# Cached keys gathered during the first attention, transposed by VectorE, kept in DRAM and loaded transposed in the second

## What is computed

```python
x = x + _L1_attn_ref(_L1_cond_ref(x, lens, conv_w), w_qkv, w_o)          # attention 1: 32 heads, 8 key heads, d=128
x = x + _L1_ffn_ref(_L1_cond2_ref(x, Wq, Wk, Wv, Wo, ..., k_cache, v_cache, block_table, cache_seqlens), ...)

def _L1_cond2_ref(...):                                                   # attention 2: the same heads, with a paged cache
    q, k = _rope(_rmsnorm(x @ Wq.T), pos), _rope(_rmsnorm(x @ Wk.T), pos)
    v = x @ Wv.T
    kc = k_cache[block_table].reshape(bsz, 512, HK, D)                    # 16 pages of 32 keys for each sequence
    vc = v_cache[block_table].reshape(bsz, 512, HK, D)
    k_all, v_all = concat([kc, k], 1), concat([vc, v], 1)                 # 512 cached + 128 own keys
    scores = einsum('bqhd,bkhd->bhqk', q, repeat(k_all)) * SCALE          # cached keys at or past cache_seqlens masked
    o = einsum('bhqk,bkhd->bqhd', softmax(scores), repeat(v_all))
    return o @ Wo.T
```

## Time and profile before

| | |
|---|---|
| time, median of 3 runs | 2040.61 us (2037.54 to 2041.23) |
| time of the profiled execution | 2036.61 us, its span 2034.7 us |
| mean granted TensorE clock | 0.999 |
| busy: PE, DVE, ACT, POOL | 1986.8, 1534.6, 1324.8, 805.8 us |
| start of attention 2 (first L1629) | 889.02 us |

### The profile page before, as it was taken

One profiled execution on the slowest core, in us unless ns is written; L12 is line 12 of the kernel. 1 busy time (PEld: TensorE's weight loads), 2 busy tenths in 40 slices (PEclk: granted clock), 3 DMA queues, 4 the chain that ended last, 5 costly groups with the idle time before them and its releaser, 6 DMA issues.

```text
span 2034.7 us, 35876 instructions
## 1 busy us (share of the span) xinstructions
PE 1986.8 (98%) x12477; PEld 1695.1 (83%) x12477; DVE 1534.6 (75%) x3383; ACT 1324.8 (65%) x3796; POOL 805.8 (40%) x797
## 2 busy tenths in 40 slices
PE   6999999999999999999999999999999999999997
PEld 5778677888888888888888888888888888888774
DVE  6777764556656555687887888878878888888998
ACT  4676763445554544576776777767767767777785
POOL 3200015100000000056666666666666666666662
PEclk9999999999999999999999999999999999999999
DMA  7301101101201110121111111211211111112010
GB/s 261 99 28 48 53 1 73 62 32 37 68 32 39 56 53 1 58 79 31 62 53 31 63 51 32 71 44 36 80 32 63 53 32 62 53 31 83 26 31 37
DMA packets 45011, 108.62 MB, mean 53 GB/s; under 512 B 15634, under 2 KB 21010, under 8 KB 40354
## 3 DMA queue, kind: packets, MB, share of 16 engines
q1 hardware_dynamic: 28450, 72.74, 10.3%
q0 software_dynamic: 16384, 33.59, 5.6%
HBM read 103.14 MB, written 3.15 MB: 52 GB/s over the span
## 4 chain that ended last, share of the span: by engine, by line
PE 91%; DVE 4%; ACT 3%; issue 1%; DMA 1%; SPq 0%; DVEq 0%; ACTq 0%
PE PS L1662 10%; PE PS L1487 9%; PE PS L1430 9%; PE PS L1566 9%; PE PS L1674 8%; PE PS L1629 7%; PE PS L1647 7%; PE PS L1580 4%; PE PS L1443 4%; PE PS L1632 3%; PE PS L342 3%; PE PS L1458 3%; PE PS L1473 2%; PE PS L498 1%; PE PS L1465 1%; PE PS L1598 1%
## 5 line engine op out<-in xcount | busy, mean ns | idle before, releaser
L2528 POOL DMA_INDIRECT kcache<-in_kcache,rows x256 | 249.6, 975 | 533.1 <-DVE x_res L1829 462.4
L2536 POOL DMA_INDIRECT vcache<-in_vcache,rows x256 | 257.2, 1005 | 124.2 <-issue 58.4
L2002 DVE CUSTOM_DVE_ANT_0 pr<-PS,ffn_weights,sm 128x640 f32<-128x640 f32 x256 | 224.6, 885 | 87.5 <-PE PS L1632 87.5
L2387 ACT ACTIVATE pr<-pr,sm 128x640 f32<-128x640 f32 x256 | 212.5, 830 | 40.1 <-DVE sm L2002 39.3
L2018 DVE TENSOR_TENSOR prT_lo<-PS,prT_hi 128x512 fp32r<-128x512 f32 x320 | 209.2, 686 | 37.0 <-ACT prT_hi L2398 30.8
L2398 ACT ACTIVATE prT_hi<-PS 128x512 fp32r<-128x512 f32 x320 | 178.0, 597 | 61.1 <-PE PS L1647 60.5
L1647 PE MATMUL PS<-consts,pr 128*128 128x128 f32 x1280 | 172.3, 273 | 2.2 <-DVE prT_lo L2018 1.7
L1647 PEld LDWEIGHTS PS<-consts,pr 128*128 128x128 f32 x1280 | 149.7, 141 | 26.3 <-DVE prT_lo L2018 2.7
L2542 POOL TENSOR_TENSOR vcached_lo<-vcache,vcached_hi 128x512 fp32r<-128x512 f32 x64 | 83.7, 1308 | 218.7 <-ACT vcached_hi L2370 218.7
L1629 PE MATMUL PS<-kT_hi,qT_hi 128*128 128x320 f32 x512 | 154.4, 309 | 2.5 <-DVE sm L2002 1.2
L1629 PE MATMUL PS<-kT_lo,qT_hi 128*128 128x320 f32 x512 | 154.1, 309 | 0.0
(11 more groups left out here) (321 smaller groups left out, 6178.1 us busy)
## 6 DMA issues: line engine op xcount, KB each, us to landing
arena<-in_wqkv SPq DMA_DIRECT2D x16, 1536.0 KB, 6.5
arena<-in_wo SPq DMA_DIRECT2D x16, 1024.0 KB, 5.4
arena<-in_wcT SPq DMA_DIRECT2D x8, 1024.0 KB, 6.7
kcache<-in_kcache,rows POOLq DMA_INDIRECT x256
vcache<-in_vcache,rows POOLq DMA_INDIRECT x256
arena<-in_xT SPq DMA_DIRECT2D x8, 256.0 KB, 7.8
x_res<-in_x SPq DMA_DIRECT2D x1, 2048.0 KB, 13.5
ffn_weights<-in_alibi SPq DMA_DIRECT2D x2, 1024.0 KB, 7.1
```

What stands on the lines that cost most here:

```text
L2002: dve.tensor_tensor_reduce(pr2[:, h, :].rearrange("p (a n) -> p a n", a=2), PS[:, SCORE_BANK[h]:SCORE_BANK[h] + 2, 0:HALF], keymask[:, b, ...
L2387: act.activation(pr2[:, h, :], pr2[:, h, :], ACT.Exp, bias=nm2[:, h:h + 1], scale=-1.0, accum_out=rs2[:, h:h + 1]).then_inc(a2_ex, 1)
L2528: pool.indirect_dma_start(out=kcache[:, c, :], out_offset=None, in_=T["kcache"], in_offset=bass.IndirectOffsetOnAxis(ap=rows[:, g, b, c:c ...
L2536: pool.indirect_dma_start(out=vcache[:, c, :], out_offset=None, in_=T["vcache"], in_offset=bass.IndirectOffsetOnAxis(ap=rows[:, g, b, c:c ...
```

## The change

The cached keys are gathered during attention 1, in another order of rows, so that four 32x32-block transposes by VectorE make columns that a transfer can put in place; the transposed keys are written to DRAM by GpSimd (`turned_kept`) and loaded by SP into `kcache` in attention 2, already transposed.

- **GpSimd**: after the tables, `pool_turned_keys`: for each of the 64 items a gather of four indirect transfers into `key_pages` (two buffers), and a store of 256 KB from `key_turned` (two buffers, both in the part of `ffn_weights` where the masks come later). `pool_masks` follows it and now waits until all 64 stores have landed. In `pool_paged`, `load_keys` is gone, and `lo_of_cached_k` is now GpSimd's, once an item.
- **DVE**: `turn_keys` at the end of items 5 to 61 of attention 1, once an item and twice in every eighth one; `lo_of_cached_k` is gone from attention 2.
- **ACT**: `hi_of_cached_k` reads `kcache` in SBUF where it read bank 3. The first stands in item 62 of attention 1, before it stood in item 63.
- **PE**: no `turn_cached_k`. The output product of attention 2 is in bank 3 but for the last item; it waits for the second row maximum where it waited for the fourth; its other waits stay. The scores' wait for the adding of the product moved from head 0 to head 1.
- **SP**: four small transfers more at the start (page numbers in the other order, each read as 32 copies of 32 single numbers); four transfers of 64 KB an item in attention 2; the weights of attention 2 are issued between them.

```diff
+            for q in range(4):
+                sp.dma_start(key_page_i[q * 32:(q + 1) * 32, :],
+                             T["pages"].rearrange("c (b q) -> q (c b)", q=CHUNKS)[q, :].partition_broadcast(32),
+                             allow_slow_non_contiguous=True).then_inc(s_setup, 16)
...
+        FIRST_TURN, LAST_TURN = GH + 1, ITEMS - 3
+        def turns_in(i):
+            if not FIRST_TURN <= i <= LAST_TURN:
+                return range(0)
+            first = i - FIRST_TURN + (i - FIRST_TURN + B - 1) // B
+            return range(first, min(first + 1 + (i % B == FIRST_TURN), ITEMS))
+
+        def pool_turned_keys(pool):
+            def gather(n):
+                g, b = group_of(n)
+                wait(pool, s_kpt, n - 1)
+                wait(pool, s_kpg, 16 * CHUNKS * n)
+                for c in range(CHUNKS):
+                    pool.indirect_dma_start(out=key_pages[:, n % 2, c, :], out_offset=None, in_=T["kcache"],
+                                            in_offset=bass.IndirectOffsetOnAxis(ap=key_rows[:, g, c, b:b + 1], axis=0)
+                                            ).then_inc(s_kpg, 16)
+            def store(n):
+                pool.wait_ge(s_kpt, n + 1)
+                wait(pool, s_kps, 16 * n)
+                pool.dma_start(turned_kept[n, :, :, :].rearrange("r p n -> p r n"),
+                               key_turned[:, n % 2, :, :, :].rearrange("p r c n -> p r (c n)")).then_inc(s_kps, 16)
...
+            gather(0)
+            gather(1)
+            for n in range(ITEMS):
+                store(n)
+                if n + 2 < ITEMS:
+                    gather(n + 2)
+
         def pool_masks(pool):
-            pool.wait_ge(a1_xT, B)
+            pool.wait_ge(s_kps, 16 * ITEMS)
...
+            def load_keys(n):
+                wait(sp, a2_kcl, n)
+                for r in range(4):
+                    sp.dma_start(kcache[32 * r:32 * (r + 1), :, :],
+                                 turned_kept[n, r, :, :].rearrange("(a j) n -> j a n", j=32)).then_inc(a2_kg, 16)
+            load_weights2(0)
+            sp.wait_ge(s_kps, 16 * ITEMS)
...
-                elif i == ITEMS - 2:
-                    turn_cached_k(0)
...
                 if i + 1 < ITEMS:
-                    pe.wait_ge(a2_max, 4 * (i + 1) + 4)
+                    pe.wait_ge(a2_max, 4 * (i + 1) + 2)
                 for h in range(GH):
                     for j, (a, c) in enumerate(PARTS):
-                        mm = pe.matmul(bank(0), o2[a][:, h, :], w_out[c][:, h, :],
+                        mm = pe.matmul(bank(OUT_BANK[i + 1 == ITEMS]), o2[a][:, h, :], w_out[c][:, h, :],
...
-                    turn_cached_k(i + 1)
...
+            def turn_keys(n):
+                dve.wait_ge(s_kpg, 16 * CHUNKS * (n + 1))
+                wait(dve, s_kps, 16 * (n - 1))
+                dve.transpose(key_turned[:, n % 2, :, :, :].rearrange("p r c n -> p c r n"),
+                              key_pages[:, n % 2, :, :].rearrange("p c (r n) -> p c r n", r=4)).then_inc(s_kpt, 1)
...
             def hi_of_cached_k(n):
-                act.wait_ge(a2_kcT, n + 1)
-                act.activation(kT2[0][:, 0:CACHED], bank(3), ACT.Copy).then_inc(a2_kch, 1)
+                act.wait_ge(a2_kg, 16 * 4 * (n + 1))
+                wait(act, a2_sc, GH * n)
+                act.activation(kT2[0][:, 0:CACHED], kcache[:].rearrange("p c d -> p (c d)"), ACT.Copy).then_inc(a2_kch, 1)
...
+            def lo_of_cached_k(n):
+                pool.wait_ge(a2_kch, n + 1)
+                pool.tensor_tensor(kT2[1][:, 0:CACHED], kcache[:].rearrange("p c d -> p (c d)"), kT2[0][:, 0:CACHED],
+                                   ALU.subtract).then_inc(a2_kcl, 1)
```

More of the change, by code:

```diff
@@ L1249, in build @@
         SCORE_BANK = 0, 2, 4, 0
+        OUT_BANK = 3, 0
         QPARTS = KT + 1
@@ L1352, in sp_attentions, with load_weights2 @@
             sp.wait_ge(a1_wol, GH * G)
-            for g in range(G):
+            def load_weights2(g):
                 wait(sp, a2_wl, QPARTS * g)
@@ L1582, in project_kv @@
                 mm.then_inc(a2_kv, 1)
-            def turn_cached_k(n):
-                pe.wait_ge(a2_kg, 16 * CHUNKS * (n + 1))
-                if n == 0:
-                    pe.wait_ge(a1_kTc, ITEMS)
-                for c in range(CHUNKS):
-                    mm = pe.transpose(bank(3, P, c * P), kcache[:, c, :], ident)
-                mm.then_inc(a2_kcT, 1)
             def turn_q(n):
@@ L1610, in scores @@
                 for h in range(GH):
-                    if h == 0:
+                    if h == 0 and i == 0:
+                        pe.wait_ge(a1_max, ITEMS)
+                    if h == 1:
                         wait(pe, a2_acc, i - 1)
-                        if i == 0:
-                            pe.wait_ge(a1_max, ITEMS)
                     if h == 2 and i == 0:
@@ L1903, in step1 @@
                         lo_of_out_weights1(g, h)
+                for n in turns_in(i):
+                    turn_keys(n)
             def row_steps(step, inv, rows):
@@ L2522, in pool_paged @@
             ch = Chain(pool, s_chp, counted["pool"])
-            def load_keys(n):
-                g, b = group_of(n)
-                wait(pool, a2_kcT, n)
-                for c in range(CHUNKS):
-                    pool.indirect_dma_start(out=kcache[:, c, :], out_offset=None, in_=T["kcache"],
-                                            in_offset=bass.IndirectOffsetOnAxis(ap=rows[:, g, b, c:c + 1], axis=0)
-                                            ).then_inc(a2_kg, 16)
+            def lo_of_cached_k(n):
+                pool.wait_ge(a2_kch, n + 1)
+                pool.tensor_tensor(kT2[1][:, 0:CACHED], kcache[:].rearrange("p c d -> p (c d)"), kT2[0][:, 0:CACHED],
+                                   ALU.subtract).then_inc(a2_kcl, 1)
             def load_values(n, cs=range(CHUNKS)):
@@ L2628, in _ @@
             pool_tables(pool)
+            pool_turned_keys(pool)
             pool_masks(pool)
```

77 lines of the change are left out of this document (46 added, 31 removed).

## The result

The changed kernel takes 2085.06 us in the median of 4 runs (2082.49 to 2087.63), the kernel before 2039.64 in those rounds; the ratio is 1.0223, with a 95% interval from 1.0204 to 1.0242. The profiled execution has a span of 2079.7 us, 45.0 more than before.

What follows compares the result with a forecast made beforehand. TensorE was taken as the bound, but in attention 2 waiting for VectorE's low part. 2036.61 + 14.4 (junction) + 3 (start) - 1 (last items) = 2053.0, so a median of 2057, range 2050 to 2066 (0.62).

Steps and rivals of the forecast that it cites:

- Start: Kernel start: four new transfers of 1024 single numbers delay sequence 1's inputs; 3 us taken, between 0 and 38.
- My own rival with a start of 10 to 20 us: Kernel start: the new transfers cost 10 to 20 us instead of 3, total 2064 to 2074; chance 0.08.
- Gathers, transposes and stores in attention 1: Attention 1: VectorE's transposes fit its idle time and GpSimd's rounds fit 8.1 us each; cost taken as 0.
- Junction: Between the attentions: eight masks behind the last store delay item 0's factors, so attention 2 begins 14.4 us late.
- the slow landing: Junction: last store landing 5.4 us after issue, like the quantised weights', rather than 2.0; attention 2 then 18 us late.
- Steady item of attention 2: Attention 2: removing four transposes gains 0.00, since the output product still waits for VectorE's low part; 0.43 us becomes a wait.
- The 27 us of the rival: Attention 2: the removed transposes' 0.43 us is real, so 62 items save 27 us, giving 2030; chance 0.11.
- End: Last items of attention 2: the chain passes elsewhere there, so 1 us comes off (0 to 4).
- GpSimd as the bound of attention 1: Attention 1: a store costs 3.9 us, 64 rounds take 589 us against 522, 67 us slower, 2124; chance 0.10.
- Gathers slowing VectorE: Attention 1: gathers slow VectorE where GpSimd was idle, needing over 3.0 us an item; 2060 to 2078; chance 0.03.
- three signs of being wrong: Attention 2 item shorter by over 0.1 us, store issue over 2.8 us, or item 0's factors ready before 895.
- What would show it: Expected signs, among them: sequence 1's wait at 26.01 grows about 3 us; items of attention 1 keep their length.

Runs made afterwards that it cites:

- The runs with the steps: Changed kernel with the 1024 row steps stored as eight transfers of 128: 2106.80 us; with their one store moved behind attention 2's third load of keys: 2078.80 us.
- the masks apart: Changed kernel with GpSimd making mask 0 ahead of the last store and the other seven one by one in items 0 to 6 of attention 2: 2071.80 us.
- The needless transposes: Changed kernel with four transposes of a constant put in each item of attention 2 where the turns of the cached keys stood: 2083.18 us.
- the kernel before with the moved low part: Kernel before with only VectorE's low part of the last output moved ahead of the fourth row maximum: 2043.33 us, ratio 1.0002.

## Why the prediction was wrong

- **Start, predicted 3 (0 to 38), measured 17.7.** The step that failed: "Between 0 and 38 I take 3, near the issue cost." I had priced each transfer at its issue of 0.95 us, as that of the page numbers, which are contiguous rows; the nearest row in form was the 4 KB in single numbers with its 11.6 us, and I set it aside with "transfers overlap". Four of that form held the queue for some 4.6 us each. The Trainium skill (DMA: Bandwidth & Descriptors, Rules for kernel authors), which makes one descriptor of each element, had spoken against it; the trace agrees with 13.71 us of issue against 4.09. My own rival with a start of 10 to 20 us has the size, but I gave it 0.08, and its 2064 to 2074 lack the 9.3 us of the next term.
- **Attention 1, predicted 0, measured 9.3.** The second step that failed: the term "Gathers, transposes and stores in attention 1 ... Taken: 0". The prices of its parts were right: a transpose 0.70 us, a store 0.80, a round of GpSimd within 8.1. What was missing is that the change makes landings in attention 1 urgent that were not before, within a few us, and that an old store of 1024 single numbers stands in that stretch. I quoted its 11.6 us in the earlier trace rows as a price and did not ask what else was in flight with it. The runs with the steps show it: 7.1 us there, some 2 of them the clock behind the wait, and nothing if moved to attention 2. The other 2.2 us in four items are waits for VectorE, where a transpose stands ahead of the probabilities; not tested by themselves.
- **Junction, predicted 14.4, measured 14.7.** The steps held one by one: last transpose near 873.5 and, with the 27 us by then, 900; landing 2.0 us after the store's issue; masks 19.7 for 18.7; factors behind them. With the masks apart 10.2 of the 14.7 come back in the trace. The order of what waits behind was right too, but a second limit of 4 us lies under it. Part of the closeness is luck: by the terms as they stand 877 + 18.7 + 5.3 gives 901.0 and 14.1 us, and 17.1 instead of 18 for the slow landing.
- **Steady item of attention 2, predicted 0, measured 0.00**, with the idle time where it was named (0.38) and VectorE's end 0.05 ahead. The needless transposes show it; the kernel before with the moved low part agrees, but there the fourth maximum holds the product too. The 27 us of the rival were there to be had only with one more edit, and then as 16.5 to 18.
- **End, predicted -1, measured +3.0.** The last six items gave 0.6 back; the two pauses of GpSimd, for which no row of before spoke, took 3.3.
- **Rivals.** GpSimd as the bound of attention 1 did not come: 0.80 us, not 3.9. The Trainium skill (DMA: Bandwidth & Descriptors, Anatomy of one DMA, SWDGE path), by which many descriptors cost little to emit, agrees. (The prediction's bound of "about 522 us" is not what its rows give: 872.87 less 343.50 is 529, and two items less 511, or 8.0 a round; at the measured 7.1 nothing hung on it.) Gathers slowing VectorE did not show: its operations of attention 1 took 0.69 us in both kernels.

The direction was right; the sum missed 28 us: 14.7 at the start (17.7 less 3), 9.3 in attention 1 and 4.0 at the end (3.0 against -1), and its own range covered neither of the first two. None of the three signs of being wrong that I had named came up (a shorter item, a dear store, early factors); what failed stood under "What would show it", in the wait for sequence 1 and in the items of attention 1. Most of the 28 are transfers of single numbers, once new at the start, once old and newly in the way, and they hurt in two ways: the loads at the start by their number, some 4.6 us for each 1024, the store by itself, with a price that hardly depends on the number. The same page of the Trainium skill gives 512 bytes as the least size for full rate and says that below it the engines read, modify and write back (Specifications). The late landing of the store fits that, without showing what the engines do inside; but the runs of 256 bytes near 489 in the changed kernel are below 512 too, and they held up nothing.

## What to carry to other kernels

When work that awaits transfers is moved into a stretch, list everything else in flight there and its form, not only its bytes: a store of single numbers that nobody waits for made the landings near it some 10 us late. Price a transfer by the row that has its form, however inconvenient that row is. When matmuls are removed and nothing is won, look at what TensorE waits for in the gap and move that ahead; here neither was worth anything without the other, and together they were worth 0.34 us an item. And a list of waits has a least size: a wait of 0.12 us in each item did not stand in it.

## What the runs showed of the hardware

- A store of 1024 single numbers to DRAM landed 11.6 us after its issue with nothing behind it in flight, though its last packet had passed after 4.7. Behind it in attention 1 packets of 4096 bytes took 1.8 to 2.7 us instead of 0.2, for some 7 us in all with the milder ones; after 256 numbers, as two stores, they took up to 3.5 for some 5 us. In attention 2 a load of 1.5 MB landed after 18.3 us instead of 7.1.
- Four loads of 1024 single numbers took SP 13.71 us to issue, and the small one behind them 4.63, in all some 4.6 us for each 1024; the first three landed 4.8 us apart.
- VectorE's transpose of 128x512 float32 in 32x32 blocks took 0.70 us, like its plain operations of that size. GpSimd's direct store of 256 KB took 0.80 us to issue, less than a gather of 64 KB.
- The clock granted to TensorE was at the lower of its two levels from 31.3 to 48.4 us in the changed kernel, where it stood idle from 26.0 to 45.3, and again from 792.5 to 799.3, from 908.5 to 911.9 and from 922.2 to 932.4, each time with idle time of TensorE just before; the kernel before kept the upper level, 2.4 GHz, from 13 to 2020 us.
